# Gate scores as extra columns of the shared low-rank tile, token rows turned from the summed x, and the exponential between gelus

## The reference

```python
xt = einsum('bct,bcd->bdt', x, weights[conditions])      # tokens, (1024, 256)
probs = softmax(xt @ gate_w)                             # 8 experts
top_p, top_i = top_k(probs, 2)
# each expert takes its first 160 first choices and 160 second choices
h = gelu(buf @ w1[e] + b1[e])                            # 256 -> 1024
y = h @ w2[e] + b2[e] + gelu(buf @ wd[e]) @ wu[e]        # low-rank path of rank 32
out = sum over both choices of p * y[token's place]
sh = gelu(xt @ sw1 + sb1) @ sw2 + sb2 + gelu(xt @ swd) @ swu
result = x + out + 0.2 * sh
```

## Time and profile before

| | |
|---|---|
| median of 3 runs | 193.1 us (193.08 to 193.26) |
| the profiled execution's own time | 193.34 us |
| its span, first to last instruction | 191.6 us |
| busy: PE, DVE, ACT, POOL | 182.3, 137.3, 137.5, 106.9 us |
| mean granted clock of PE | 0.992 of full |

### The profile page before, as it was taken

How to read it: one execution, slowest core, us unless ns; L and a number is a source line. 1 busy time by engine, 2 the same in 40 slices (tenths; PEclk the granted TensorE clock), 3 DMA queues, 4 the chain that set the end, 5 groups by cost and what they waited for, 6 DMA issues and landing times.

```text
span 191.6 us, 3982 instructions
## 1 busy us (share of the span) xinstructions
PE 182.3 (95%) x1410; PEld 174.5 (91%) x1410; DVE 137.3 (72%) x297; ACT 137.5 (72%) x291; POOL 106.9 (56%) x118
## 2 busy tenths in 40 slices
PE   6999999999999999999999999999999999999950
PEld 6996788998889999999999999999999999999850
DVE  4389489796455276695795896897897896879710
ACT  2256899306959306996996997998997989899400
POOL 5400005899817470140688688688788770747380
PEclk9999999999999999999999999999999999999996
DMA  4593500069903222827668767978968949851442
GB/s 145 147 331 99 205 19 0 0 227 311 317 14 96 72 68 38 294 68 248 209 74 259 225 120 226 253 127 232 248 126 246 293 56 274 233 58 14 56 43 33
DMA packets 23816, 29.23 MB, mean 153 GB/s; under 512 B 4442, under 2 KB 20564, under 8 KB 23796
## 3 DMA queue, kind: packets, MB, share of 16 engines
q1 hardware_dynamic: 19412, 23.03, 38.2%
q0 software_dynamic: 4016, 5.38, 17.5%
q10 hardware_dynamic: 368, 0.56, 1.0%
HBM read 23.92 MB, written 5.05 MB: 151 GB/s over the span
## 4 chain that ended last, share of the span: by engine, by line
PE 70%; DMA 9%; POOL 5%; DVE 4%; ACT 4%; issue 3%; SPq 2%; POOLq 1%; DVEq 0%
PE hid_ps L909 10%; PE hid_ps L911 10%; PE hid_ps L910 10%; PE y_ps L911 10%; PE y_ps L910 10%; PE y_ps L909 10%; POOL out_rows L408 5%; DMA out_rows<-y_row,slot_tok 4%; DMA gate_raw<-in_L_ffn_gate_w 3%; DMA wu_raw<-in_L_ffn_b 2%; PE turn_ps L1077 2%; ACT gelu_f L558 2%; ACT hid_h L559 1%; DVE w_l L622 1%; PE hid_ps L930 1%
## 5 line engine op out<-in xcount | busy, mean ns | idle before, releaser
L651 DVE TENSOR_TENSOR hid_l<-gelu_f,hid_h 128x320 fp32r<-128x320 f32 (+1 forms) x80 | 41.8, 534 | 19.0 <-ACT hid_h L559 18.5
L408 POOL DMA_INDIRECT out_rows<-y_row,slot_tok x24 | 41.5, 1730 | 13.4 <-DVE y_row L830 6.6
L394 POOL DMA_INDIRECT slot_in<-slot_rows,slot_src x24 | 31.7, 1320 | 21.2 <-PE turn_ps L1077 10.0
L909 PE MATMUL hid_ps<-xs_h,w_h 128*128 128x256 f32 (+2 forms) x128 | 37.9, 296 | 0.0
L558 ACT ACTIVATE gelu_f<-hid_ps,bias_s 128x320 f32<-128x320 f32 x64 | 34.8, 544 | 2.6 <-PE hid_ps L911 1.1
L910 PE MATMUL hid_ps<-xs_l,w_h 128*128 128x256 f32 (+2 forms) x128 | 36.6, 286 | 0.0
L911 PE MATMUL hid_ps<-xs_h,w_l 128*128 128x256 f32 (+2 forms) x128 | 36.6, 286 | 0.0
L909 PE MATMUL y_ps<-w_h,hid_h 128*128 128x256 f32 x128 | 36.3, 284 | 0.0
L910 PE MATMUL y_ps<-w_l,hid_h 128*128 128x256 f32 x128 | 36.2, 283 | 0.0
L911 PE MATMUL y_ps<-w_h,hid_l 128*128 128x256 f32 x128 | 36.2, 283 | 0.0
L559 ACT ACTIVATE hid_h<-hid_ps,bias_s 128x320 fp32r<-128x320 f32 x64 | 35.0, 547 | 0.0
(11 more groups left out here) (209 smaller groups left out, 375.2 us busy)
## 6 DMA issues: line engine op xcount, KB each, us to landing
w_raw<-in_L_ffn_w SPq DMA_DIRECT2D x16, 1024.0 KB
x_in<-in_x SPq DMA_DIRECT2D x2, 512.0 KB, 4.7
w_raw<-in_L_ffn_sw SPq DMA_DIRECT2D x1, 1024.0 KB
slot_rows<-token_row SPq DMA_DIRECT2D x2, 512.0 KB, 4.0
out_rows<-base SPq DMA_DIRECT2D x2, 512.0 KB
wu_raw<-in_L_ffn_wu SPq DMA_DIRECT2D x24, 32.0 KB
w_raw<-in_L_ffn_sw ACTq DMA_DIRECT2D x1, 512.0 KB
w_raw<-in_L_ffn_sw SPq DMA_DIRECT2D x1, 512.0 KB, 5.2
```

What stands on the lines that cost most here:

```text
L394: pool.indirect_dma_start(out=slot_in[par][0:n, s, :], out_offset=None, in_=x_rows, in_offset=bass.IndirectOffsetOnAxis(ap=slot_src[0:n, e ...
L408: pool.indirect_dma_start(out=out, out_offset=bass.IndirectOffsetOnAxis(ap=slot_tok[0:n, e, s:s + 1].bitcast(U32), axis=0), in_=y_row[0:n, ...
L651: dve.tensor_tensor(hid_l[:, j - 1, 0:n], gelu_f[:, j % 3, 0:n], hid_h[:, j - 1, 0:n].bitcast(F32), ALU.subtract).then_inc(hid_split, 1)
L909: pe.matmul(out_ap, l_h, r_h, start=start, stop=False)
```

## The change

- **Scores.** The high and low parts of the gate's eight columns become columns 96 to 111 of the shared low-rank tile (`low_gate_h`, `low_gate_l`; they lie in `xs_h` and `xs_l`, which are free then). Tile j = 0 of both halves is made first, half 1's in the bank `turn_ps[1]`, and DVE copies rows 96 to 111 of it as the scores. `score` is gone, with its eight matmuls.
- **Token rows.** POOL adds `xct_h` and `xct_l` (four sums of 128x512 into `base`, at that time unused), and PE turns the sums behind half 0's hidden tiles (sixteen turns of 128x128), each group when the gelus have freed its bank. ACT copies the rows behind the last gelu of half 0.
- **Exponential.** It stands behind gelu 2 of half 0 (`EXP_AT = 2`); a gelu of one column at the start brings the gelu table in ahead of everything. The count stands behind tile 7, the slot map behind tile 6 of half 1.
- **w2 of the shared expert.** POOL casts it; DVE's four subtractions stand behind all nine splits of half 0, and PE waits for them one by one in the first shared output.
- **Half 1 and the next weights.** ACT casts the first expert's w1 behind gelus 5 to 8 of half 1, and DVE's subtractions stand behind splits 5 to 8. `gelu_tile(1, 0)` waits until half 0's outputs are done, as they still read `low_s`.

```diff
-COUNT_AT = 4
+COUNT_AT = 7
+EXP_AT = 2
+MAP_AT = 6
+LOW_GATE = LOW + 2 * E
...
+        low_gate_h, low_gate_l = [x[:, :, 0:LOW_GATE] for x in (xs_h, xs_l)]
+        xct_f = base[:, :, :].rearrange("p t f -> p (t f)").rearrange("p (k n) -> p k n", k=KD)
...
         def hid_ring(u):
-            return hid_ps + [row_ps, y_ps[1], turn_ps[1]] if u == 0 else hid_ps
+            return hid_ps + [row_ps, y_ps[1], y_ps[0]] if u == 0 else hid_ps
 
         def hid_bank(u, j):
-            return hid_ring(u)[j % len(hid_ring(u))]
+            return turn_ps[1] if u == 1 and j == 0 else hid_ring(u)[j % len(hid_ring(u))]
+
+        token_bank = [row_ps] + hid_ps
...
             wd_hi_part(0, 0)
+            for h in range(2):
+                cols = slice(h * HALF, (h + 1) * HALF)
+                for k in range(KD):
+                    pool.wait_ge(xct_lo, h * KD + k + 1)
+                    pool.tensor_tensor(xct_f[:, k, cols], xct_h[:, k, cols].bitcast(F32), xct_l[:, k, cols].bitcast(F32),
+                                       ALU.add).then_inc(xct_summed, 1)
+            pool.wait_ge(w2_in, 16)
+            for c in range(CHUNKS):
+                pool.tensor_copy(w2_h[0][:, c * FT:(c + 1) * FT, :],
+                                 w2_raw[:, c * FT:(c + 1) * FT, :]).then_inc(w2_hi, 1)
             wu_hi_part(0, 0)
...
+            act.wait_ge(warm_set, 1)
+            act.activation(warm_act[:, :], warm_act[:, :], ACT.Gelu)
             act.wait_ge(gate_in, 16)
-            act.activation(gate2[:, :, 0:E], gate_raw[:, :, :], ACT.Copy).then_inc(gate_hi, 1)
+            act.activation(low_gate_h[:, :, LOW:LOW + E], gate_raw[:, :, :], ACT.Copy).then_inc(gate_hi, 1)
...
-            copy_rows(0)
-            w2_chunk(0, 0, 0)
-            copy_rows(1)
-            w2_chunk(0, 0, 1)
-            copy_rows(2)
-            copy_rows(3)
-            for c in range(CHUNKS // 2, CHUNKS):
-                w2_chunk(0, 0, c)
-            act.wait_ge(centred, 1)
-            act.activation(expd[:, :, :], logits[:, :, :], ACT.Exp).then_inc(expd_made, 1)
...
             for j in range(HT):
                 gelu_tile(0, j, HALF, shared_bias)
+                if j == EXP_AT:
+                    act.wait_ge(centred, 1)
+                    act.activation(expd[:, :, :], logits[:, :, :], ACT.Exp).then_inc(expd_made, 1)
...
-            for c in range(CHUNKS):
-                w1_chunk(1, 1, c)
+            for b in range(NT // 2):
+                copy_rows(b)
             for j in range(HT):
                 gelu_tile(1, j, HALF, shared_bias)
+                if j >= HT - CHUNKS:
+                    w1_chunk(1, 1, j - (HT - CHUNKS))
...
+            dve.memset(low_gate_l[:, :, LOW:LOW_GATE].bitcast(F32), 0.0)
...
-            for c in range(CHUNKS // 2):
-                w2_chunk(c, 0, 0)
+            split_tile(0, 0, HALF)
+            split_tile(0, 1, HALF)
...
+            split_tile(0, 2, HALF)
             choose(0)
+            split_tile(0, 3, HALF)
             choose(1)
+            dve.engine_nop().then_inc(chosen_made, 1)
+            split_tile(0, 4, HALF)
             make_values()
-            for j in range(HT):
+            wu_part(0, 0)
+            for j in range(5, HT):
                 split_tile(0, j, HALF)
...
+            for c in range(CHUNKS):
+                w2_chunk(c, 0, 0)
             place_tokens()
...
             def make_rows(b):
+                pe.wait_ge(xct_summed, KD * (b * 2 // HTILES + 1))
+                last = HT - NT // 2 + b
+                pe.wait_ge(hid_gelu, hid_count(0, 3 if b == 0 else last))
                 for t in (2 * b, 2 * b + 1):
-                    ins = pe.matmul(row_banks[b][:, (t % 2) * D:(t % 2 + 1) * D], cond_diag[:, t, :], x_in[:, t, :],
-                                    start=True, stop=True)
+                    for k in range(KD):
+                        ins = pe.transpose(token_bank[b][:, (t % 2) * D + k * P:(t % 2) * D + (k + 1) * P],
+                                           xct_f[:, k, t * P:(t + 1) * P], ident[:, :])
...
+            hidden(0, 0, 0, 0, xct_h, xct_l, half_cols[0], HALF)
+            hidden(1, 0, 0, 0, xct_h, xct_l, half_cols[1], HALF)
             for h in range(2):
...
-                for j in range(HT):
...
+                for j in range(1, HT):
...
                     hidden(h, j, 0, 0, xct_h, xct_l, cols, HALF)
+                    if h == 0 and j == 1:
+                        gate_tokens()
```

More of the change, by code:

```diff
@@ L258, in hid_before, with wd_pair, made_count @@
             return v * HT
+        def wd_pair(v, par):
+            if v > 0:
+                return wd_h[par][:, :, :, :], wd_l[par][:, :, :, :]
+            return [w[:, :, 0:LOW].rearrange("p k (g r) -> p k g r", g=3) for w in (low_gate_h, low_gate_l)]
+        def made_count(u, j):
+            if u == 1 and j == 0:
+                return 2
+            return hid_count(u, j) + (1 if u == 0 and j > 0 else 0)
         def hid_ring(u):
-            return hid_ps + [row_ps, y_ps[1], turn_ps[1]] if u == 0 else hid_ps
+            return hid_ps + [row_ps, y_ps[1], y_ps[0]] if u == 0 else hid_ps
         def hid_bank(u, j):
-            return hid_ring(u)[j % len(hid_ring(u))]
+            return turn_ps[1] if u == 1 and j == 0 else hid_ring(u)[j % len(hid_ring(u))]
+        token_bank = [row_ps] + hid_ps
         rows_bank = [y_ps[0], y_ps[1], row_ps]
@@ L605, in _ @@
         def _(dve):
+            dve.memset(warm_act[:, :], 0.0).then_inc(warm_set, 1)
             dve.memset(wu_raw[LOW:P, :], 0.0).then_inc(rows_zero, 1)
@@ L988, in hidden @@
                     pe.wait_ge(wd_lo, v + 1)
-                if u > 0 or j >= len(hid_ring(0)):
+                if u < 2 and j == 0:
+                    pe.wait_ge(gate_lo, 1)
+                    pe.wait_ge(xct_lo, (u + 1) * KD)
+                elif u > 0 or j >= len(hid_ring(0)):
                     pe.wait_ge(hid_gelu, hid_count(u, j) - len(hid_ring(u)))
-                m = 3 * RANK if j == 0 else P
+                m = P if j > 0 else LOW if u > 1 else LOW_GATE
                 dst = hid_bank(u, j)[0:m, 0:n]
                 for k in range(KD):
-                    if j == 0:
+                    if j == 0 and u < 2:
+                        l_h, l_l = low_gate_h[:, k, :], low_gate_l[:, k, :]
+                    elif j == 0:
                         l_h, l_l = (w[:, k, :, :].rearrange("p g r -> p (g r)") for w in (wd_h[par], wd_l[par]))
@@ L1016, in shared_out @@
                 for f in range(NF):
+                    if n == 0 and f % FT == 0:
+                        pe.wait_ge(w2_lo, f // FT + 1)
                     if t == 0:
@@ L1106, in map_slots @@
                 ins.then_inc(map_made, 1)
+            half_cols = [slice(h * HALF, (h + 1) * HALF) for h in range(2)]
+            hidden(0, 0, 0, 0, xct_h, xct_l, half_cols[0], HALF)
+            hidden(1, 0, 0, 0, xct_h, xct_l, half_cols[1], HALF)
             for h in range(2):
-                cols = slice(h * HALF, (h + 1) * HALF)
-                for j in range(HT):
-                    if h == 0 and j < 2:
-                        pe.wait_ge(scores_copied, j + 1)
-                    if h == 0 and j == 2:
+                cols = half_cols[h]
+                for j in range(1, HT):
+                    if h == 1 and j == 1:
                         pe.wait_ge(rows_copied, NT // 2)
                     hidden(h, j, 0, 0, xct_h, xct_l, cols, HALF)
+                    if h == 0 and j == 1:
+                        gate_tokens()
                     if h == 0 and j == COUNT_AT:
                         count_before()
-                    if h == 1 and j == 5:
+                    if h == 1 and j == MAP_AT:
                         map_slots()
+                if h == 0:
+                    for b in range(NT // 2):
+                        make_rows(b)
                 for t in range(HTILES):
```

65 lines of the change are left out of this document (20 added, 45 removed).

## The result

The change makes the kernel slower. The median of nine runs is 193.87 us (193.39 to 194.15), that of before on the same chip 193.08 (192.90 to 193.26, nine runs): a ratio of 1.0033, with a 95% interval of 1.0025 to 1.0041. (The ratios of this document are those on record and differ a little from the quotients of the medians, here 1.0041.) The profiled execution took 193.75 us with a span of 192.0, against 193.34 and 191.6.

A forecast was written before the change was run, and what follows sets the result against it. PE was taken to bound the kernel. Gain 0.82 - 0.10 - 0.06 - 0.20 = 0.46, say 0.5 us: profiled 193.34 becomes 192.84, and the median, 0.24 below the profiled run, 192.6; range 191.8 to 194.2.

The forecast's parts named there:

- Table loads: ACT, half 0: exponential between two table loads of 1.28 us each, so gelu 3 starts at 25.63.
- Rival C: ACT's table changes each cost 1.38 us more than the load, 2.8 in all: slower, 195.4; 5 in 100.
- Tile (1,0)'s wait: PE waits 0.15 us for the low part of half 1 before its low-rank tile, which runs from 16.47.
- The count's wait: PE, behind tile (0,7), waits from 28.3 to 29.45 for DVE's second choice: a new wait of 1.15 us.
- The first output's: PE's first shared output of half 0 waits 0.9 us for the first w2 low piece, behind split 8 on DVE.
- Net at tile (1,1): 0.82 earlier: At half 1's first wide tile, 3.6 us of saved PE work less 2.8 of waits leaves 0.82 us.
- Rival B: POOL's second sum precedes DVE's waiting w1 piece; tile (1,0) and gelus 1.8 us later: slower, 194.2; 13 in 100.
- I take 0.1 lost: Half 1: split 8 ends at 61.5, where the output's last product asks for it at 61.6; 0.1 us lost.
- 3 us of room for the third, hidden: Gathers start later, from 58.35 and 1.3 apart; PE wants them at 65.1, so the third has 3 us: no loss.
- rival F: First gathers land after 65.1, starting 1.4 later and meeting the moved w1 load: 1 us wait, 193.6; 5 in 100.
- Rival D: No change: POOL's hold on DVE costs 0.4 to 0.6, half 1's late split 0.2: 192.9 to 193.3; 20 in 100.
- Rival E: The added-up waits overlap better than charged at hand-overs between engines: about 1.2 us gained, 191.9; 10 in 100.

The follow-up runs named there:

- The tail part alone: Kernel before with w1 pieces behind gelus and splits 5 to 8 of half 1, map and DVE's wd and wu parts one tile later: 193.47 us, 1.0015.
- the second series: The changed kernel measured again, unedited, beside the variants on one chip: 194.03 us, ratio 1.0038 to the kernel before.
- POOL's wait: Changed kernel with POOL's four sums and what follows held back until DVE's four shared-expert w1 pieces are done: 193.27 us, 1.0001.
- all at once: Changed kernel with POOL waiting and casting w2 first, exponential behind gelu 1, map at 5, w2, w1 pieces and splits 2, 3 moved: 193.60 us, 1.0030.
- the load out of the way: Changed kernel with SP's w1 load for the second expert waiting for the turn of the gathered rows: 193.99 us, 1.0043.

## Why the prediction was wrong

The forecast was 192.6, faster; it is 193.87, slower by 0.33%. The time lies inside the range, the direction is wrong.

- **Work taken off PE** (3.6 net): right, 3.5 on the page.
- **Table loads** (gelu 3 at 25.63): right. It is at 26.06, or 26.26 by the old head; the hold of 0.43, which that figure did without, is most of the rest, and it was late before the first load. Rival C is out: with it gelu 3 would have run at 28. The Trainium skill's drain of 1.38 us (ScalarE: Activation LUTs, What ACT_TABLE_LOAD costs) does not show at either load.
- **Tile (1,0)'s wait** (0.15): 0.55, the hold again. **The count's wait** (1.15): right, 1.19. **The last turns' wait** (0.4): 0.29. **The first output's** (0.9): 0.59 by the list, 0.8 to 0.9 when it was removed.
- **"Net at tile (1,1): 0.82 earlier", less 0.2 for the hold: the step that failed.** Measured: 0.02 earlier, so 0.60 is missing. By the old head (0.20 is added to after's times) it can be followed. The hold was priced at 0.2 and is 0.43: the w1 piece takes 1.11 instead of 0.68, and putting the sums behind it gave 0.42 back. That is 0.23. Gelu 2 was laid out 0.04 behind the end of its tile; tile (0,3) starts at 21.71 and the gelu at 21.91, 0.20 behind. That is 0.16. Both pass unchanged through gelu 3 (0.63 late), the count (30.06 instead of 29.45) and the first w2 product (34.95 instead of 34.35). Last, "begin in effect at 34.1" was 0.25 ahead of that product, though one matmul of 0.12 gives only 0.12, and the product after a wait costs 0.22 (34.75 to 34.97) instead of 0.12: another 0.23. These make 0.62, against 0.60. The first is shown by an experiment, the other two are read from the timeline alone. The 45.73 that I took from the chain is 45.56 on the timeline, but it stands in the sum only with the 46.27 worked out from it and changes nothing in the 0.82. For the hold I had chosen a case near "0.15 lost" where a cast of 0.39 was the other side; a sum of 1.48 holds longer.
- **Rival B** (POOL's second sum goes ahead, tile (1,0) at 18): no. DVE's piece did not wait for the second sum: it began at 14.25, with about 0.76 of the first sum still to run (an estimate, from 13.53 and the mean of 1.48), and lost 0.43. The Trainium skill (SBUF — State Buffer, Who interferes with whom) says that a DVE instruction with two SBUF inputs contends with a GpSimd one that reads SBUF, and that one with at most one SBUF input doesn't, outside the modes that use both ports. The runs agree on both: 0.68 became 1.11 and 0.22 became 1.20 with two, and the pair with one input in PSUM kept its 1.28.
- **"I take 0.1 lost" behind half 1, and "3 us of room for the third, hidden": failed.** Measured: 0.6 at the first expert. Split 8 ends at 62.16, which is 2.68 behind half 1's first output, as laid out, and the wait for it costs 0.2. The room was 4.15 by the prediction's own times (65.1 less 58.35 and twice 1.3), and is 3.64, as the gathers start 1.38 and 1.62 apart; but the third one's rows come after 3.93, and that costs another 0.34 in that trace. It is the gather's late start of rival F (5 in 100, about 1 us) and a third of its size; that the load has a part in it, as F had it, is not shown. The tail part alone, in the kernel before, has the ratio 1.0015.
- **Rival D** named two of the right causes, the hold of 0.4 to 0.6 and the late split of 0.2, and ended at 193.3; with the gather's 0.34 on top it is 193.6. Rival E, that the waits overlap, did not happen: each stood nearly at its forecast size.
- **The shift at the turn of the rows reaches the end**: right. The first expert's first tile is 0.61 later relative, the end of the span 0.60. The 0.06 in front can't be told, as the first token product starts anywhere from 10.81 to 11.12 in these traces.

So of the 1.27 us between 192.6 and 193.87, 0.60 was lost ahead of half 1 and 0.51 behind it (0.61 less the 0.1 that was forecast). The reason behind it: a gain of 0.46 was what was left of 3.6 after four waits. Its error was the sum of their errors.

Open: why the changed kernel's runs lie 0.8 to 1.9 us apart (193.39 to 194.15, and 193.15 to 195.05 in the second series) and before's nine 0.4, though before had single runs of 195.33 and 195.03 in later series. With the map back at 5 they lie within 0.6, but so they do with POOL's wait and the map at 6, and all at once, map at 5, they lie 1.2 apart; with the load out of the way 2.0. A gather whose landing varies fits some of this and not well the rest. The traces show one execution each, so it is not settled. Likewise whether the w1 load slows the gathers. It goes out 0.90 behind the start of the third gather both in the changed kernel and with the exponential one gelu earlier, and the gathers between 55 and 67 us have landings with medians of 4.0 us in one trace and 3.1 in the other. So the load alone does not tell the two apart.
